# An expert stage in 63 units of 128 rows, two to a turn, in place of 35 tiles of 256 rows

## What is computed

```
xt = layernorm(x).reshape(3584, 256)
w, idx = top_k(xt @ Wg.T + bg, 2);  w = softmax(w)
h = relu(xt @ W1[e].T + b1[e])        # 256 -> 512, per expert e
y = h @ W2[e].T + b2[e]               # 512 -> 256
x = x + sum over the two chosen e of w[e] * y[e]
```

## Time and profile before

| | us |
|---|---|
| median of three runs (1064.32 to 1065.72) | 1064.37 |
| the profiled execution, its own time | 1060.8 |
| its span in the trace | 1059.0 |
| PE matmul busy | 959.3 (91%) |
| DVE busy | 763.2 (72%) |
| ACT busy | 552.9 (52%) |
| POOL busy | 564.6 (53%) |
| mean granted TensorE clock | 0.97 |

### The profile page before, as it was taken

One profiled execution on the slowest core, in us unless ns is written; L12 is line 12 of the kernel. 1 busy time (PEld: TensorE's weight loads), 2 busy tenths in 40 slices (PEclk: granted clock), 3 DMA queues, 4 the chain that ended last, 5 costly groups with the idle time before them and its releaser, 6 DMA issues. The chain is left out here.

```text
span 1059.0 us, 31414 instructions
## 1 busy us (share of the span) xinstructions
PE 959.3 (91%) x10666; PEld 675.3 (64%) x10666; DVE 763.2 (72%) x2164; ACT 552.9 (52%) x1090; POOL 564.6 (53%) x904
## 2 busy tenths in 40 slices
PE   4799999999999999988799999999963699999993
PEld 2466666666666666656456666666642588888872
DVE  4688788887888888894768888888765266666553
ACT  3566666666666666655224444444442355555541
POOL 6655454555545555410126777777776355555444
PEclk9999999999999999998799999999997799999997
DMA  5644344444444344322355656555561355555443
GB/s 153 174 136 135 104 121 122 136 110 123 118 127 136 110 122 120 108 79 83 104 151 166 187 189 194 181 179 184 182 197 58 119 91 90 98 96 92 83 63 41
DMA packets 104687, 134.03 MB, mean 127 GB/s; under 512 B 23713, under 2 KB 93873, under 8 KB 104369
## 3 DMA queue, kind: packets, MB, share of 16 engines
q1 hardware_dynamic: 90994, 113.93, 36.6%
q0 software_dynamic: 13536, 18.10, 10.1%
HBM read 93.80 MB, written 38.73 MB: 125 GB/s over the span
## 5 line engine op out<-in xcount | busy, mean ns | idle before, releaser
L991 DVE TENSOR_REDUCE smax<-psum 112x2 f32<-112x750 f32 x240 | 221.2, 934 | 45.8 <-PE psum L443 44.5
L823 ACT ACTIVATE probsT<-psum 125x896 f32<-125x896 f32 x173 | 158.8, 918 | 54.7 <-PE psum L458 53.4
L1963 POOL DMA_INDIRECT out_dram<-y,token_at x70 | 111.9, 1599 | 112.0 <-DMA out_dram<-y,token_at 53.5
L2044 ACT ACTIVATE h<-psum,b 128x256 f32<-128x256 f32 x140 | 58.7, 470 | 99.5 <-PE psum L1991 99.5
L1718 DVE SCALAR_TENSOR_TENSOR acc<-psum,neg_bias,acc 128x448 f32<-128x448 f32 x112 | 75.8, 679 | 10.8 <-PE psum L1542 10.7
L443 PE MATMUL psum<-k_stack,q_stack 63*128 63x375 f16 x480 | 78.5, 326 | 3.5 <-DVE smax L991 0.7
L478 PE MATMUL psum<-probsT,v_aug 125*32 125x112 f32 x2688 | 81.6, 262 | 0.0
L1461 POOL DMA_INDIRECT dispatch_dram<-rows,slots_at x64 | 64.0, 1000 | 28.4 <-issue 28.4
L1542 PE MATMUL psum<-xT_hi,we_hi 128*128 128x448 f16 x256 | 70.2, 356 | 1.1 <-ACT we_hi L1640 1.1
L396 POOL CAST k_hi<-we 128x375 f16<-128x375 f32 x64 | 31.9, 498 | 73.6 <-ACT we L843 73.5
L458 PE MATMUL psum<-q_stack,k_stack 64*128 64x112 f16 x1384 | 64.2, 212 | 7.3 <-DMA q_stack<-neg_max 2.7
(11 more groups left out here) (277 smaller groups left out, 2455.6 us busy)
## 6 DMA issues: line engine op xcount, KB each, us to landing
k_stack<-k_hi_dram SPq DMA_DIRECT2D x64, 188.0 KB, 2.8
we<-in_ctxT_dram SPq DMA_DIRECT2D x32, 375.0 KB, 3.7
ctxT<-in_ctxT_dram SPq DMA_DIRECT2D x32, 375.0 KB
ctx_rows<-in_ctx_dram SPq DMA_DIRECT2D x32, 375.0 KB
rows_e<-dispatch_dram SPq DMA_DIRECT2D x70, 136.0 KB, 2.4
w_raw<-in_w_dram SPq DMA_DIRECT2D x32, 256.0 KB, 3.8
k_hi_dram<-k_hi SPq DMA_DIRECT2D x32, 188.0 KB, 3.2
k_lo_dram<-k_lo SPq DMA_DIRECT2D x32, 188.0 KB, 3.4
```

Of the source, the lines that this page charges most:

```text
L823: nc.scalar.activation(probsT[:, p, c, hg, :, :, :].rearrange("p k h q -> p k (h q)"), psum[0:KC, 0:2, 0:4 * S], ACT.Exp, scale=float(HD) ...
L991: nc.vector.reduce_max(smax[:, (u - LAG_B) % 2, 2 * (s % 4) + s // 4::PAIRS], psum[0:S, pair_bank(s):pair_bank(s) + 2, 0:KV], AX.X).then_i ...
L1963: nc.gpsimd.indirect_dma_start(dram["out"], bass.IndirectOffsetOnAxis(token_at[:, n % 2, s:s + 1], 0), y[:, n % 2, s, :], None, compute_op ...
L2044: nc.scalar.activation(h[:, c, :], psum[:, 1 + c // 2, (c % 2) * TILE:(c % 2 + 1) * TILE], ACT.Relu, bias=b1[:, c, bass.ds(e, 1)]).then_in ...
```

## The change

The unit of work is 128 rows (`UNIT`), each with an expert of its own. There are NU = 63 units in the order of experts, spare ones last; a turn has two of them (`PAIR`), the last turn one, so there are 32 turns. TensorE does `up` for both units of a turn, then `turn_rows` of the next turn, then `down` for both units of the turn before. All is still written out in Python.

- An `up` of a unit has 24 matmuls that move 128 columns, so a turn has 48. A `down` of a unit has the 12 matmuls of a half, so a turn has 24, as before. Each unit looks up its own expert on TensorE and on VectorE; ScalarE looks up one for each turn.
- Bias and relu of the second unit are moved from ScalarE to VectorE (`second_hidden`, four instructions of 128 by 128). High and low parts of the hidden values are made in one instruction for a unit.
- The copies `meta` and `weight` are gone; the token's weight is read straight from the loaded row. Row buffers are held until `y` is done, and token numbers have four buffers, so that copy waits for no scatter. `y` has four slots, and writing a slot waits for the scatter of four units before.
- A scatter waits always for the one two units back, and for the one just before it only where an expert begins.
- Padding rows are no longer scattered by GpSimd in the expert phase: SyncE looks up eight start rows and writes them with eight plain DMAs at the end of the middle phase, and waits for them there.
- Four more plain DMAs of padding stand in SyncE's queue at the start of the middle phase. The table needs 16 instructions of VectorE where it took 27.

The diff, cut to its core:

```diff
-TILE = 256
-NT = (2 * TOKENS + E * (TILE - 1)) // TILE
+UNIT = 128
+NU = (2 * TOKENS + E * (UNIT - 1)) // UNIT
+SPARE = 4
...
-            for n in range(2):
-                sp.dma_start(dram["dispatch"][DUMMY + n * 128:DUMMY + (n + 1) * 128, :], dram["pads"][n]).then_inc(m["pads_out"], 16)
-            for n in range(3):
+            for n in range(SPARE):
+                sp.dma_start(dram["dispatch"][DUMMY + n * UNIT:DUMMY + (n + 1) * UNIT, :], dram["pads"][n]).then_inc(m["pads_out"], 16)
+            for n in range(SPARE + 1):
...
-            sp.wait_ge(m["pads_out"], 16 * 5)
             sp.wait_ge(m["late_in"], 16 * len(keep["late_loads"]))
+            sp.wait_ge(m["table"], 2)
+            for e in range(E):
+                start = sp.value_load(pad_start[0:1, e:e + 1], min_val=0, max_val=DISPATCH_ROWS - UNIT)
+                sp.dma_start(dram["dispatch"][bass.ds(start, UNIT), :], keep["pad_rows"][:]).then_inc(m["pads_out"], 16)
+            sp.wait_ge(m["pads_out"], 16 * (2 * SPARE + 1 + E))
...
-            for e in range(E):
-                nc.gpsimd.indirect_dma_start(dram["dispatch"], bass.IndirectOffsetOnAxis(pad_at[:, e:e + 1], 0),
-                                             pad_rows[:], None).then_inc(m["pads_sent"], 16)
+            for unit in range(NU):
+                before = look_up(pool, 2, unit, 16, landed(NU)) if unit >= FREE_FROM else landed(unit - 1)
+                wait(pool, m["y_rdy"], unit + 1)
+                if unit > 1:
+                    pool.wait_ge(added[(unit - 2) % SLOTS], landed(unit - 2))
+                if unit > 0:
+                    pool.wait_ge(added[(unit - 1) % SLOTS], before)
+                nc.gpsimd.indirect_dma_start(dram["out"], ..., y[:, unit % SLOTS, :], None, compute_op=ALU.add).then_inc(added[unit % SLOTS], 16)
...
+            def up(n, s, e, then):
+                if s == 0:
+                    wait(pe, m["xlo_rdy"], n + 1)
                 for c in range(HC):
                     if c % 2 == 0:
+                        wait(pe, h_rdy[s], HC * (n - 1) + c + 2)
                     else:
                         then(c)
                     done = 0
                     for w, x in ((w1_hi, x_hi), (w1_hi, x_lo), (w1_lo, x_hi)):
                         for kc in range(DC):
+                            last = nc.tensor.matmul(up_bank(s, c),
                                                     w[:, bass.ds(e, 1), kc, c * 128:(c + 1) * 128].rearrange("p o h -> p (o h)"),
+                                                    x[:, n % 2, kc, s * UNIT:(s + 1) * UNIT], start=(done == 0), stop=(done == 3 * DC - 1))
...
+            def down(n, s, e):
+                wait(pe, hlo_rdy[s], n + 1)
+                wait(pe, y_sum_rdy[s], n)
+                for hh, w in ((h_hi, w2_hi), (h_hi, w2_lo), (h_lo, w2_hi)):
+                    for kc in range(HC):
+                        last = nc.tensor.matmul(psum[:, 5 + s, 0:D], hh[:, n % 2, s, kc, :],
+                                                w[:, bass.ds(e, 1), kc, :].rearrange("p o d -> p (o d)"), ...)
...
             turn_rows(0)
+            for n in range(TURNS):
+                for s in units(n):
+                    up(n, s, expert[PAIR * n + s], next_expert(n, s))
+                if n + 1 < TURNS:
                     turn_rows(n + 1)
                 if n > 0:
+                    for s in units(n - 1):
+                        down(n - 1, s, expert[PAIR * (n - 1) + s])
...
+            for n in range(TURNS):
+                tokens(n)
+                if len(units(n)) > 1:
+                    second_hidden(n, e[1])
+                low_h(n, 0)
+                if n + 1 < TURNS:
+                    low_x(n + 1)
+                if len(units(n)) > 1:
+                    low_h(n, 1)
                 if n > 0:
+                    for s in units(n - 1):
+                        finish(n - 1, s, before[s])
```

More of the change, by code:

```diff
@@ L1628, in _ @@
             pe.wait_ge(m["table"], TABLE_OPS)
-            for n in range(4):
-                last = nc.tensor.matmul(psum[0:1, 1, n * NT:(n + 1) * NT], tile[:, n:n + 1], ident[0:NT, 0:NT], start=True, stop=True)
+            for n in range(3):
+                last = nc.tensor.matmul(psum[0:1, 1, n * NU:(n + 1) * NU], unit_row[:, n:n + 1], ident[0:NU, 0:NU], start=True, stop=True)
             last.then_inc(m["tally_done"], 1)
@@ L1853, in _ @@
-            dve.wait_ge(table_sem, 12)
-            nc.vector.tensor_reduce(run(ends), upto_length, AX.X, ALU.add).then_inc(table_sem, 1)
+            nc.vector.tensor_scalar(later, starts, unit_no[:], None, ALU.is_gt).then_inc(table_sem, 1)
+            nc.vector.scalar_tensor_tensor(base, starts, -float(UNIT), expert_row[:], ALU.mult, ALU.add).then_inc(table_sem, 1)
+            dve.wait_ge(table_sem, 8)
+            nc.vector.scalar_tensor_tensor(own, ends, unit_no[:], later, ALU.is_gt, ALU.subtract).then_inc(table_sem, 1)
@@ L1857, in _ @@
             dve.wait_ge(table_sem, 14)
[L1858 to L1878, removed]
+            nc.vector.tensor_scalar(unit_row[:, 1:2], unit_row[:, 1:2], unit_spare[:], None, ALU.add).then_inc(table_sem, 1)
@@ L1918, in expert_phase @@
-    m = {n: sem("x_" + n) for n in names}
-    rows_in = [m[f"rows_in{n}"] for n in range(ROW_BUFS)]
-    added = [m["added0"], m["added1"]]
-    def apart(engine):
-        engine.sem_inc(m["passed"], 1)
-    def look_up(engine, what, n, least, most):
-        return engine.value_load(table[0:1, what, n:n + 1], min_val=least, max_val=most)
-    def rows_arrived(n):
-        return 16 * HALF * (n // ROW_BUFS + 1)
-    def landed(n):
-        return LANDED * (n // 2 + 1) if n >= 0 else 0
+    PAIR = 2
@@ new lines, in expert_phase @@
+    TURNS = -(-NU // PAIR)
+    ROW_TURNS = 4
+    SLOTS = 4
+    FREE_FROM = SLOTS + 1
+    b1, b2, table = (keep[k] for k in ("b1", "b2", "table"))
+    rows = sb("rows_e", [128, ROW_TURNS, PAIR, ROW], F32)
+    token_at = sb("token_at", [128, ROW_TURNS, PAIR], U32)
+    x_hi = sb("x_hi", [128, 2, DC, PAIR * UNIT], F16)
+    x_lo = sb("x_lo", [128, 2, DC, PAIR * UNIT], F16)
+    h = sb("h", [128, PAIR, HC, UNIT], F32)
+    h_hi = sb("h_hi", [128, 2, PAIR, HC, UNIT], F16)
+    h_lo = sb("h_lo", [128, 2, PAIR, HC, UNIT], F16)
@@ new lines, in expert_phase, with units, look_up, up_bank @@
+    up_done, h_rdy, hhi_rdy, hlo_rdy, down_done, y_sum_rdy = (
+        [m[f"{k}{s}"] for s in range(PAIR)] for k in ("up_done", "h_rdy", "hhi_rdy", "hlo_rdy", "down_done", "y_sum_rdy"))
+    def units(n):
+        return range(min(PAIR, NU - PAIR * n))
+    def look_up(engine, what, unit, least, most):
+        return engine.value_load(table[0:1, what, unit:unit + 1], min_val=least, max_val=most)
+    def up_bank(s, c):
+        return psum[:, 1 + 2 * s + c // 2, c % 2 * UNIT:(c % 2 + 1) * UNIT]
@@ L1968, in _ @@
+            for unit in range(NU - SLOTS, NU):
+                pool.wait_ge(added[unit % SLOTS], landed(unit))
         @block.tensor
@@ L2056, in low_x @@
             def low_x(n):
+                width = len(units(n)) * UNIT
                 wait(dve, m["xhi_rdy"], n + 1)
[L2058 to L2066 removed]
@@ new lines, in tokens, with experts @@
+            def tokens(n):
+                wait(dve, rows_in[n % ROW_TURNS], rows_arrived(n))
+                nc.vector.tensor_copy(token_at[:, n % ROW_TURNS, 0:len(units(n))].rearrange("p (n o) -> p n o", o=1),
+                                      rows[:, n % ROW_TURNS, 0:len(units(n)), AT_TOKEN:AT_TOKEN + 1]).then_inc(m["token_rdy"], 1)
+            def experts(n):
+                return [look_up(dve, 0, PAIR * n + s, 0, E - 1) for s in units(n)]
+            low_x(0)
+            before, e = None, experts(0)
@@ L2101, in build @@
+            for s in units(TURNS - 1):
+                finish(TURNS - 1, s, before[s])
 def build(nc, dram):
```

301 lines of the change are left out of this document (129 added, 172 removed).

## The result

The changed kernel took **1093.99 us** (median of 4 runs, 1091.19 to 1095.68) against 1064.34 for the kernel before on the same chip: ratio **1.0288, 95% interval 1.0253 to 1.0323**. Forecast were 1084.5 with a range of 1052 to 1096: the direction and the mechanism came true, and the size was 9.5 us too small, which leaves the result 2 us inside the upper end of the range. The profiled execution took 1092.74 us with a span of 1090.9; the granted clock was 1.00 throughout the turns.

The account below looks back on a forecast made before the run. TensorE's instruction queue was to bound the turn: first turn 7.4, thirty of 7.5 (225), last 11.4, together 243.8 against 230.0 (plus 13.8); start plus 6.3, so plus 20.1 us, median 1064.4 to 1084.5, range 1052 to 1096.

Parts of the forecast that it names:

- TensorE's queue: Step on TensorE's instruction queue in a turn: doubled register work, two look-ups and waits, no longer hidden; 7.4 us, taken as 7.5.
- The bound of 7.8: Upper limit set on the turn's time from the work of TensorE's instruction queue: 7.8 us, against 7.5 taken.
- The tail: Last `up` to the end of the span: `up`, three `down`, matmul tail, VectorE, scatter and landing; 11.4 us.
- The start: Padding in SyncE's queue ahead of the middle phase's end delays the expert phase: plus 6.3 us (5 to 8).
- Array: TensorE's array in a turn: 128-column `up` matmuls at 57 ns, plus transposes and `down`; 5.77 us needed.
- chain over x: Two `up` (5.1 us), then transposes, `x_hi`, `x_lo` and handing over (2.3 us): 7.4 us a turn, no third bound.
- VectorE's 6.3 us: VectorE's work in a turn, 5.0 us plus two look-ups: 6.3 us, under 7.5, costing nothing; next bound if the queue were free.
- the queue's work stays hidden: Rival: register operations cost TensorE's queue only bare durations, the array's 5.77 us bounds turns; minus 32.5 us, 1031.9; chance 0.10.
- Unhidden loads: Rival: 98 ns weight loads never hidden behind `up` matmuls, a turn of 7.75 us; plus 28 us, 1092; chance 0.04.
- The case in between: Rival: VectorE's 6.3 us or something up to 7.1 bounds the turn; at 6.7, minus 4 us, 1060; chance 0.14.
- The clock did not halve: Rival: TensorE's clock halves in gaps of `up`, a turn of 11.5 us, 1220; chance 0.02 together with scatters still waiting.
- The `out_dram` waits: Expected sign in the profile: GpSimd's waits for its scatters no longer in the chain; 21 us of waiting go.

## Why the prediction was right, and where its sizes were off

*What the change loses.* The step "TensorE's queue" carries the result, and its claim that nothing hides it any more is shown from both sides: without address work the change is 2.5% faster than the kernel before, and the address work alone makes the kernel before 5.2% slower.

*The turn, 7.5 forecast and 7.76 measured.* The 0.118 us for a register operation, the price this term rests on, was too low, and over 30 turns the term is 7.7 us short. The usual steps are right (0.113 and 0.124, mean 0.118). But now and then one takes up to 0.295, which brings the mean to 0.125: 48 x 0.007 = 0.34 us a turn. Both short stretches from which I took 0.118 held no such step. A mean over many turns of the kernel before was not to be had that way, as the queue waits there. The four waits and the look-ups came as forecast, 0.45 and 1.31 against 0.48 and 1.30. The bound of 7.8 took this in.

*The tail, 11.4 forecast and 15.05 measured.* The prediction had written "the wait for the one two units back needs 4.9 us within a turn of 7.5: hidden". True in the turns and false in the tail, where the last three `y` come 1.0 and 1.4 us apart (1080.55, 1081.55, 1082.91). Unit 62's scatter waits for unit 60's to land (at 1085.97), and that one had itself started 1.8 us behind its `y`: it waited for unit 58's until 1080.94, 0.4 us, and its issue came 1.4 us behind that wait. Up to the last `y` the forecast fits (7.06 against 6.9); the 3.5 us behind it are this wait.

*The start.* Plus 6.3 forecast, plus 6.7 measured (829.01 to 835.72), and the split of the padding confirms its place.

*Array, chain over x, VectorE.* 5.77 us for the array became 5.75 in the run with split columns. The chain over x at 7.4 became 7.54 once the queue was relieved. VectorE's 6.3 us was sized 0.3 too high: it holds the turn of 5.99 once the queue is free. It cost nothing in the change, as forecast.

*The rivals.* That the queue's work stays hidden would have given 1031.9; the run that takes the work away gave 1038.69, so this rival's price was about right and its condition false. Unhidden loads gave the right turn by coincidence, and the run with fixed weights tells the two apart. The case in between (a turn of 6.7) did not come. The clock did not halve: the granted clock was 1.00 with TensorE busy 92% of the turns.

*One sign that did not come.* The `out_dram` waits were to leave the chain; they still lead it with 3%, and 28.3 us of them are left. That cost TensorE nothing in the turns, since its queue stands at no wait there.

*The fit to the median.* I had carried over that the profiled execution lies 3.6 us under the median; here it was 1.25 under. So of the 11.8 us that the profiled execution is longer than forecast, the median shows 9.5. That part is luck: with the old distance the median would have been 1096.3, just outside the range.

## What to carry to other kernels

When the weights of a matmul are picked by a register, count the queue's register operations for each turn (0.125 us each here, a look-up 0.65) and compare the sum with the array's time: cutting a tile in half doubles the first and leaves the second as it was. The gain of a finer order (fewer waits on scatters) can be had without the cut: here the same table and waits with the old tile size (and two copies fewer on VectorE) won 1.1% where the cut lost 2.9%. And a wait that is hidden within the turn has to be priced again for the tail, where the last results come close together.

## What the runs showed of the hardware that was not expected

- The steps of TensorE's queue have a second, longer kind. Between 880 and 960 us of the change's trace some 52 steps behind register operations were 0.02 to 0.17 us longer than the usual 0.113 or 0.124, 3.3 us in all, or 0.32 a turn. Two thirds of them lie 29 to 34 instructions behind the one before (register operations, loads and matmuls counted), most others about 40, or two or three times 32. What the queue does there was not tested.
- A load and matmul of 128 columns take 56 ns when the queue is ahead, so cutting 256 columns in two costs the array almost nothing (2.68 us for 48 against 2.62 for 24).
